# Cross-attention of a decoder layer, from pairs of heads over all tokens to units of one token tile and four heads

## The chip, the cores and the metric

One core of a Trainium2 chip runs the whole program. The time is the device's, in microseconds (us), from launch to end; the kernel before took 972.54 us (median of 3 runs, 971.64 to 976.59). The engines are PE (TensorE: products; PEld is its weight load), DVE (VectorE), ACT (ScalarE), POOL (GpSimd) and SP, which here only issues DMAs. Each engine runs its own list in order, and waits on semaphores that the others raise.

## The reference

Two sequences of 1024 tokens with 256 features pass through one decoder layer: self-attention, cross-attention on 77 context tokens and a feed-forward part, each followed by a residual sum and a layernorm without gain. The cross-attention is the part concerned:

```
q = (x @ Wq.T + bq)          # 1024 x 256, as 16 heads of 16
k = (ctx @ Wk.T + bk)        # 77 x 256
v = (ctx @ Wv.T + bv)
scores = einsum('blhd,bLhd->bhlL', q, k) / sqrt(16)
scores = where(mask, scores, -inf)       # mask 1024 x 77, all ones here
attn = softmax(scores)
out = einsum('bhlL,bLhd->blhd', attn, v) @ Wo.T + bo
x = layernorm(x + out)
```

Keys and queries are carried as two parts (hi and lo, each rounded for the fast fp32r product), so that a score is hi*hi + hi*lo + lo*hi.

## The kernel before

The two sequences (q = 0 and 1 in the code) go through the same stages one after the other: projections (stage Q), self-attention (S), cross-attention (X), norm tail (N), and the feed-forward products (F). The order of every engine's work is written out by hand: each engine walks over the same numbered steps, and in a step does its share of each part. The self-attention works on pairs of heads and chunks of 512 queries. The feed-forward products of sequence 0 are spread over the stages of sequence 1 by the table PLAN, those of sequence 1 stand at the end with a part in its norm tail. They use four PSUM banks for sequence 0 and six for sequence 1 (F_BANKS). The first feed-forward layers (w1, w2) of either sequence's first half stand in the last five steps of its own norm tail, from FFN_STEP to X_END.

Between self-attention and feed-forward stand, for each sequence:

- the norm of the self-attention, tile of 128 tokens by tile: transpose of the result (`y_to_features`), product with w_proj (`project_out`), residual, statistics and norm on DVE with the power on POOL, transpose (`x_to_features`), product with w_q (`project_q`). Tiles 0 to 3 stand beside the last steps of self-attention, tiles 4 to 7 behind it, alone.
- the cross-attention proper, in 9 leading steps and 8 main ones. In a leading step the queries of one pair of heads are split (DVE, POOL), turned by 8 transposes (`x_turn`), evacuated by ACT, multiplied with the keys once to get each query's maximum (`x_max`: a mask product and 8 products of 156 columns, in three groups), reduced on DVE (`x_reduce`), and the negated maximum is turned (`x_rows`) and written by four small DMAs into spare rows of the turned queries, so that the second product of queries and keys already holds the difference. A main step is 4 heads by 512 queries: 4 products (`x_scores`), 4 exponentials on ACT (`x_exps`), the multiplication by the mask on DVE and POOL (`x_mask`), 4 products with the values (`x_values`), an evacuation on DVE, 4 transposes (`x_y_turn`) and the division (`y_norm`).
- the norm of the cross-attention, tiles 0 to 7, which starts beside the last two main steps, and ends in the norm tail.

At the very start DVE waits for the table of cosines and the first projection and then rotates queries and keys (`rope`). The semaphore w_in counts the DMAs of the later weights; DVE, POOL and PE wait for it before self-attention.

Of the kernel before, what the change touches and what calls it, by code (L numbers as in the profile page):

```python
# [109 lines left out]
def norm_step(t):  # L110

    return (y_step(2 * NG - 2) if t < NT // 2 else FINAL_STEP - NT // 2) + 1 + t


S_END = norm_step(NT - 1) + 5
# [12 lines left out]
XSTAGE, XTURN, XMAX, XROWS = 9, 8, 7, 6  # L128
XLAST = NC * NG
XROUNDS = []  # L130
for _s in range(-XSTAGE, XLAST + 2):
    XROUNDS += [("turn", _s + XTURN, i) for i in range(2) if 0 <= _s + XTURN < NP]
    XROUNDS += [("rows", _s + XROWS, 0)] if 0 <= _s + XROWS < NP else []
    XROUNDS += [("y", _s - 2, 0)] if 0 <= _s - 2 < XLAST else []
    if _s == 0:
        XEARLY = len(XROUNDS)
XROUND_AT = {r: n for n, r in enumerate(XROUNDS)}
XUNITS = [(0, 3), (3, 3), (6, 2)]
XSHARED = 3 * XMAX
XNORM = NG + 2  # L140
FFN_STEP = XNORM + NT // 2 + 3
X_END = XNORM + NT + 4


PER = dict(
    x_t_in=16, ctx_in=80, x_in=16, rows_in0=64 * NG, rows_in1=64 * NG, xrows_in0=64 * NG, xrows_in1=64 * NG,
    filled=3, qk_mm=NT, v_mm=NT, rope_mul=3 * NT, rope_add=NT, v_evac=NT,
    ctx_mm=2, ctx_add=2, ctx_stage=3, ctx_turn=2, ctx_evac=4,
# [5 lines left out]
    xstage_hi=NP, xstage_lo=NP, xround_mm=len(XROUNDS), xturn_evac=2 * NP, xrows_evac=NP, xy_norm=2 * XLAST,  # L154
    xmax_mm=3 * NP, xmax_red=3 * NP, xmax_op=2 * NP, xscore_mm=4 * XLAST, xexp_done=4 * XLAST,
    xmask_dve=2 * XLAST, xmask_pool=2 * XLAST, xav_done=XLAST, xy_evac=XLAST,
# [13 lines left out]
XSHARED_BANKS = 6  # L170
F_BANKS = ((2, 3, 4, 5), (0, 1, 2, 3, 4, 5))


def norm_bank(k, what, t):


    if k == 0:
        if t < NT // 2:
            return {"yt": 0, "proj": 1, "xt": 0, "q": 1}[what]
        return {"yt": 0, "proj": 2, "xt": 4, "q": 6}[what] + t % 2  # L180
    return {"yt": 0, "proj": 1, "xt": 0}[what] + (6 if t >= NT // 2 else 0)


def norm_stages(k, s):

    first = [XNORM + t if k else norm_step(t) for t in range(NT)]
    lags = {"yt": 0, "proj": 1, "xt": 3} | ({} if k else {"q": 4})
    return [(what, t) for what, lag in lags.items() for t in range(NT) if first[t] + lag == s]


def bank_before(k, what, t):

    uses = [u for s in range(S_END) for u in norm_stages(k, s)]
    uses = [u for u in uses[:uses.index((what, t))] if norm_bank(k, *u) == norm_bank(k, what, t)]
    return uses[-1] if uses else None
# [11 lines left out]
SLOTS = [("N", 0, s) for s in range(FFN_STEP, X_END)] + [("Q", 1, t) for t in range(NT + V_LAG)] + \  # L207
        [("S", 1, s) for s in range(FIRST_STEP, S_END)] + [("X", 1, s) for s in range(-XSTAGE, FFN_STEP)] + \
        [("N", 1, s) for s in range(FFN_STEP, X_END)] + [("F", 1, j) for j in range(ALONE)]
# [5 lines left out]
    (0, 0, ("w1", "w2"), ("N", 0, FFN_STEP), ("N", 0, X_END - 1)),  # L215
# [7 lines left out]
    (1, 0, ("w1", "w2"), ("N", 1, FFN_STEP), ("N", 1, X_END - 1)),  # L223
# [48 lines left out]
def decoder_layer(nc, a):  # L272
    with ExitStack() as ctx:
# [7 lines left out]
        bias_q = sb("bias_q", [P, D], F32)  # L281
# [9 lines left out]
        xmask_t = sb("xmask_t", [P, T], BF16)  # L291
        kx_t = sb("kx_t", [P, NP, 2 * CP], F32R)
# [28 lines left out]
        def both(name, shape, dt, offset):  # L321
# [18 lines left out]
        kx_tok = both("kx_tok", [P, NP, 2, DH], F32, O_P + 13312)  # L340
        bias_kv = both("bias_kv", [P, 2, D], F32, O_P + 14336)
# [3 lines left out]
        qx_t = [[at(q, f"qx_t{i}", [P, T], F32R, O_T + 4096 * i if i < 6 else O_QK + 8192 + 4096 * (i - 6)) for i in range(NP)]  # L345
                for q in range(BATCH)]
# [5 lines left out]
        xmask_t_u8 = at(0, "xmask_t_u8", [CTX, T], U8, O_T + 4096)  # L352
# [28 lines left out]
        for n in "check_op flag_mm flag_set".split():  # L381
# [12 lines left out]
            x_tok=x_tok, xmask_bias=xmask_bias, xmask_t=xmask_t, xmask_t_u8=xmask_t_u8, xmask_u8=xmask_u8, y_sb=y_sb, y_t=y_t)  # L394
# [4 lines left out]
def build_layer(block, L, S):  # L399
# [41 lines left out]
    def consumer(q, rounds, n, prefix):  # L441

        kind = rounds[n][0]
        count = sum(r[0] == kind for r in rounds[:n + 1])
        name = prefix + {"turn": "turn_evac", "rows": "rows_evac", "y": "y_norm"}[kind]
        return S[name], PER[name] * q + count * (2 if kind == "y" else 1)

    def f_bank(q, n):

        return bank[F_BANKS[q][n % len(F_BANKS[q])]]  # L450

# [14 lines left out]
    def _(sp):  # L466
# [4 lines left out]
        def load_context(q):  # L471
# [4 lines left out]
            for i, n in enumerate(("bk", "bv")):  # L476
                sp.dma_start(L["bias_kv"][q][:, i], a[n].rearrange("(o n) -> o n", o=1).to_broadcast([P, D])).then_inc(S["ctx_in"], 16)
# [33 lines left out]

# [45 lines left out]
        for s in range(-XSTAGE, XLAST):  # L557
            cross_attention(0, s)
# [1091 lines left out]
```

## Time and profile before

| | |
|---|---|
| median of 3 runs | 972.54 us (971.64 to 976.59) |
| the profiled execution | 977.12 us, its span 975.2 us |
| mean granted TensorE clock | 0.914 |
| PE busy | 875.0 us (90%) |
| DVE busy | 547.5 us (56%) |
| ACT busy | 362.9 us (37%) |
| POOL busy | 361.6 us (37%) |

The span is the time from the first to the last instruction. A clock of 1.00 is 2.4 GHz, one of 0.50 is 1.2 GHz. A product's duration in the profile holds its latency too, so products in a row overlap: what one costs in a row is the distance between starts. PE is busy for nine tenths of the span, so time is gained where PE has less to do, waits less, or runs at the higher clock.

### The profile page before, as it was taken

How to read it: one execution, taken by the hardware profiler on the slowest of the kernel's cores; microseconds unless marked ns; L12 is line 12 of the kernel's file. 1: busy time of each engine (PE TensorE's matmuls, PEld its weight loads, DVE VectorE, ACT ScalarE, POOL GpSimd, SP SyncE). 2: the span in 40 equal slices, each digit the busy share in tenths (PEclk: the TensorE clock that was granted, in tenths of full speed). 3: DMA queues.
4: the chain of work that ended last, by engine and by line, in shares of the span. 5: the costliest groups of instructions: out<-in, count | busy, mean ns of one | idle time of the engine just before them, and what ended most of it. 6: DMA issues, size and time to landing. Idle time of an engine off the chain costs nothing.

```text
span 975.2 us, 13106 instructions
## 1 busy us (share of the span) xinstructions
PE 875.0 (90%) x4466; PEld 562.2 (58%) x4466; DVE 547.5 (56%) x1404; ACT 362.9 (37%) x770; POOL 361.6 (37%) x575
## 2 busy tenths in 40 slices
PE   5879999898889799989898899999988989999996
PEld 2544444234734567877666664443457367888785
DVE  4597888677676442235433488884258664117113
ACT  0315666463353322114111146665725433122110
POOL 4312323346445343424222232241343535335332
PEclk9957999769976999999999999997999599999999
DMA  9909101002200123224222105440000000000000
GB/s 330 313 5 398 56 2 45 23 1 72 96 5 0 51 98 112 93 80 152 86 87 87 44 23 183 186 153 2 1 1 6 2 1 0 1 1 23 1 1 24
DMA packets 24955, 69.37 MB, mean 71 GB/s; under 512 B 4539, under 2 KB 12680, under 8 KB 24712
## 3 DMA queue, kind: packets, MB, share of 16 engines
q1 hardware_dynamic: 24888, 68.50, 20.5%
q8 instruction: 39, 0.64, 0.3%
q14 instruction: 28, 0.23, 0.1%
HBM read 65.87 MB, written 13.63 MB: 82 GB/s over the span
## 4 chain that ended last, share of the span: by engine, by line
PE 72%; DVE 17%; POOL 4%; issue 3%; ACT 3%; DMA 1%; SPq 0%; DVEq 0%; POOLq 0%; ACTq 0%
PE bank L892 23%; PE bank L685 7%; PE bank L702 7%; PE bank L654 6%; PE bank L880 4%; DVE bank L1215 4%; DVE max_raw L1213 4%; PE bank L587 3%; PE bank L889 3%; PE bank L825 3%; PE bank L640 2%; PE bank L775 2%; PE bank L735 2%; PE bank L596 1%; POOL prob_s L1501 1%
## 5 line engine op out<-in xcount | busy, mean ns | idle before, releaser
L1530 POOL TENSOR_TENSOR hid_lo_s<-act_raw_s,hid_hi_s 128x512 fp32r<-128x512 f32 x96 | 124.0, 1292 | 211.2 <-DVE hid_hi_s L1392 186.4
L1041 ACT ACTIVATE prob_s<-bank 128x512 f32<-128x512 f32 (+3 forms) x384 | 163.7, 496 | 97.5 <-PE bank L685 97.2
L654 PE MATMUL bank<-k_t_s,q_t_s 64*128 64x512 f32 (+3 forms) x384 | 143.0, 465 | 23.0 <-DVE max_raw L1215 14.9
L1501 POOL TENSOR_SCALAR_AFFINE_SELECT prob_s<-prob_s 128x128 f32<-128x128 f32 x256 | 83.7, 345 | 164.9 <-ACT prob_s L1041 162.5
L1392 DVE CAST hid_hi_s<-act_raw_s 128x512 fp32r<-128x512 f32 x64 | 30.5, 477 | 199.5 <-ACT act_raw_s L1087 199.3
L1215 DVE CUSTOM_DVE_ANT_0 bank<-bank,causal_bf 128x128 f32<-128x128 f32 (+3 forms) x256 | 122.8, 509 | 16.9 <-PE bank L654 14.6
L685 PE MATMUL bank<-q_t_s,k_t_s 64*128 64x512 f32 (+3 forms) x384 | 118.9, 421 | 1.5 <-DVE resid_f_s L1356 0.6
L1087 ACT ACTIVATE act_raw_s<-bank,scales 128x512 f32<-128x512 f32 x64 | 43.8, 689 | 178.4 <-PE bank L892 178.4
L685 PEld LDWEIGHTS bank<-q_t_s,k_t_s 64*128 64x128 f32 x384 | 60.5, 201 | 79.5 <-ACT prob_s L1041 47.9
L654 PEld LDWEIGHTS bank<-k_t_s,q_t_s 64*128 64x128 f32 x384 | 65.6, 205 | 67.8 <-DVE max_raw L1215 31.4
L1213 DVE TENSOR_REDUCE max_raw<-bank 128x1 f32<-128x512 f32 x128 | 82.2, 683 | 39.8 <-PE bank L654 39.8
L892 PE MATMUL bank<-hid_hi_s,home_s 128*128 128x512 f32 x256 | 100.0, 391 | 3.6 <-POOL hid_lo_s L1530 3.5
L892 PE MATMUL bank<-hid_lo_s,home_s 128*128 128x512 f32 x256 | 99.6, 389 | 0.0
L702 PE MATMUL bank<-prob_s,v_sb_s 128*32 128x512 f32 (+3 forms) x768 | 91.4, 551 | 8.0 <-POOL prob_s L1501 7.7
L892 PE MATMUL bank<-hid_hi_s,ring_s 128*128 128x512 f32 x192 | 77.8, 405 | 0.0
L892 PE MATMUL bank<-hid_lo_s,ring_s 128*128 128x512 f32 x192 | 76.6, 399 | 0.0
L892 PEld LDWEIGHTS bank<-hid_hi_s,home_s 128*128 128x128 f32 x256 | 48.0, 188 | 15.4 <-issue 5.6
L892 PEld LDWEIGHTS bank<-hid_lo_s,home_s 128*128 128x128 f32 x256 | 48.1, 188 | 9.8
L1561 POOL TENSOR_TENSOR prob_s<-prob_s,xmask_t 77x512 f32<-77x512 f32 x32 | 39.1, 1240 | 35.4 <-ACT prob_s L1071 35.4
L1071 ACT ACTIVATE prob_s<-bank 77x512 f32<-77x512 f32 x64 | 32.7, 591 | 25.9 <-PE bank L813 25.8
L587 PE MATMUL bank<-w_qkv,x_t_s 128*128 128x512 f32 x64 | 32.2, 636 | 11.1 <-DMA w_qkv<-in_w_qkv 10.3
L1236 DVE COPY y_sb_s<-bank 128x512 f32<-128x512 f32 x32 | 22.1, 689 | 35.5 <-PE bank L702 17.9
(152 smaller groups left out, 1509.6 us busy)
## 6 DMA issues: line engine op xcount, KB each, us to landing
ring_s<-scratch SPq DMA_DIRECT2D x34, 512.0 KB, 3.3
home_s<-scratch SPq DMA_DIRECT2D x22, 512.0 KB, 6.0
checked_s<-scratch SPq DMA_DIRECT2D x3, 3584.0 KB, 21.6
ring_moved_s<-scratch SPq DMA_DIRECT2D x10, 512.0 KB, 3.3
x_t_s<-in_x_t SPq DMA_DIRECT2D x2, 1024.0 KB, 5.7
x_tok_s<-in_x SPq DMA_DIRECT2D x2, 1024.0 KB, 8.0
out<-tok SPq DMA_DIRECT2D x16, 128.0 KB, 1.7
q_t_s<-max_rows SPq DMA_DIRECT2D x64, 4.0 KB
```

What stands on the lines that cost most here:

```text
L587: i = mm(bank[QK_BANKS[q][t % 2]][:], x_t[q][:, k, P * t:P * (t + 1)], L["w_qkv"][:, k, 0:2 * D], start=k == 0, stop=k == KD - 1)
L654: mm(out[:, 0:k1 - k0], qkt(q, p, 0)[r, P * qt:P * (qt + 1)], qkt(q, p, 1)[r, k0:k1], start=True, stop=True).then_inc(S["max_mm"], 1)
L685: mm(S_BANK[j][:, 0:CHUNK - q0], qkt(q, p, 1)[r, P * kb:P * (kb + 1)], qkt(q, p, 0)[r, CHUNK * c + q0:CHUNK * (c + 1)], start=True, stop=T ...
L702: m = mm(Y[32 * j:32 * (j + 1), q0:CHUNK], v_window(v_sb[q][:, kb], 4 * g + j), prob[q][4 * (s % 2) + j][:, 0:CHUNK - q0], start=kb == 0, ...
L892: o = mm(out[:], view(tile_h(f_weights(q, n, 0)[:], k), True), view(src[part][:, k]), start=i == 0, stop=i == last)
L1041: act.activation(prob[q][4 * (s % 2) + j][:, 0:n], S_BANK[j][:, 0:n], ACT.Exp, scale=SCALE).then_inc(S["exp_done"], 1)
L1087: act.activation(act_raw[q][r % 3][:], f_bank(q, n)[:], ACT.Gelu, scale=scales[:, 1 + LAYER_NUMBER[layer], m:m + 1]).then_inc(S["f_act"], 1)
L1213: dve.tensor_reduce(dst, out[:], AXX, ALU.max).then_inc(S["max_red"], 1)
L1215: dve.tensor_tensor_reduce(out=out[:, 0:left], in0=out[:, 0:left], in1=L["causal_bf"][:, CHUNK - left:CHUNK], scale=1.0, scalar=NEG, op0=A ...
L1501: pool.affine_select(out=pr, in_=pr, compare_op=ALU.is_ge, fill=0.0, base=0, pattern=[[1, P]], channel_multiplier=-1).then_inc(S["select_d ...
L1530: pt(dst[1][:, m], act_raw[q][r % 3][:], dst[0][:, m].bitcast(F32), ALU.subtract).then_inc(S["f_lo"], 1)
L1561: pt(pr, pr, L["xmask_t"][0:CTX, CHUNK * (s // NG):CHUNK * (s // NG + 1)], ALU.mult).then_inc(S["xmask_pool"], 1)
```

## The change

The cross-attention works by query tiles. A unit is one token tile (128 queries) and four heads. There are 32 units for each sequence, and a step per unit. The keys are laid out once as block-diagonal matrices (`kx_blocks`, hi and lo, 64 rows by 4 x 78 columns), so that one product of the feature-major queries (64 rows, 128 queries) gives the scores of four heads, 312 columns, with the queries on the partitions. A unit is:

- PE: one mask product of 312 columns and three products (hi*hi, hi*lo, lo*hi) of 312 columns (`x_unit`)
- DVE: the maximum over each head's 77 columns, and the subtraction of it from PSUM into SBUF (`x_softmax`)
- PE, two steps later: 4 transposes of 128x77 (`x_turn`); ACT: one exponential of 77x512 (`x_exp`)
- PE, four steps later: 4 products with the values, 128 columns each (`x_values`)
- for every tile, four units: an evacuation on ACT, 4 transposes (`x_y_turn`), the division on DVE (`x_y_norm`).

The queries come feature-major out of `project_q` (four products of 128 columns instead of two of 256), and are split once, ACT writing hi and POOL lo. The leading steps, the second scores product, the rows of maxima with their DMAs and the multiplication of probabilities by the mask are gone. A query without any allowed key gets its not-a-number from `no_key`, added in the residual. The norm of the self-attention for tiles 4 to 7 stands in steps 0 to 7 of the cross-attention, and the norm of the cross-attention follows every fourth step, from step 11. The norm stages share the banks 0 and 1; the feed-forward products use four banks for both sequences. The w1 and w2 products of a sequence's first half stand in steps 33 to 43 (11 steps in place of 5). At the start the later weights' semaphore counts nine DMAs (bias and block tables are new among them), and DVE and POOL wait for it before the first rotation.

```diff
-XSTAGE, XTURN, XMAX, XROWS = 9, 8, 7, 6
-XLAST = NC * NG
-XUNITS = [(0, 3), (3, 3), (6, 2)]
-XNORM = NG + 2
-FFN_STEP = XNORM + NT // 2 + 3
-X_END = XNORM + NT + 4
+XN = NT * NG
+XTURN, XVALUES, XY = 2, 4, 2 * NG + 1
+X_NORM = XY + 2
+FFN_STEP = XN + 1
+X_END = NG * (NT - 1) + X_NORM + 5
+def norm_stages(stage, s):
+    first = {(0, t): NORM_STEP + t for t in range(NT // 2)} if stage == "S" else \
+            {(0, t): t - NT // 2 for t in range(NT // 2, NT)} | {(1, t): NG * t + X_NORM for t in range(NT)}
+    lags = {"yt": (0, 0), "proj": (1, 1), "xt": (3, 4), "q": (4, None)}
...
-F_BANKS = ((2, 3, 4, 5), (0, 1, 2, 3, 4, 5))
+XUNIT_BANKS = (2, 3)
+XTURN_BANKS = (4, 5)
+F_BANKS = (2, 3, 4, 5)
+NORM_BANKS = {"yt": 0, "xt": 0, "proj": 1, "q": 1}
...
@@ sync @@
-        for dst, name in ((L["bias_q"], "bq"), (L["bias_o"], "bo"), (L["scale_w3"], "s3")):
+        for dst, name in ((L["bias_o"], "bo"), (L["scale_w3"], "s3")):
...
-        sp.dma_start(scales[:], a["scales"]).then_inc(w_in, 16)
+        for dst, name in ((scales, "scales"), (L["bq_t"], "bq_t"), (L["bk_t"], "bk_t"), (L["blocks"], "blocks")):
+            sp.dma_start(dst[:], a[name]).then_inc(w_in, 16)
...
-        for s in range(-XSTAGE, XLAST):
-            cross_attention(0, s)
@@ tensor @@
-            for i in range(KD):
-                m = mm(out[:, 0:D], x1_t[q][t % 2][:, i], L["w_q"][:, i], start=i == 0, stop=i == KD - 1)
+            for half in range(KD):
+                for i in range(KD):
+                    m = mm(norm_bank("q")[:, P * half:P * (half + 1)], L["w_q"][:, i, P * half:P * (half + 1)], x1_t[q][t % 2][:, i],
+                           start=i == 0, stop=i == KD - 1)
...
+        def x_unit(q, n):
+            t, g = divmod(n, NG)
+            if n == 0:
+                wait(pe, q, "ctx_blocks", 4)
+                wait(pe, q, "exp_done", 4 * LAST)
+            if g == 0:
+                wait(pe, q, "q_hi", t + 1)
+                wait(pe, q, "q_lo", t + 1)
+            if n >= 2:
+                wait(pe, q, "xsub", n - 1)
+            out = x_bank(XUNIT_BANKS, n)[:, 0:4 * CP]
+            mask = L["xmask_bias"][:, t].unsqueeze(1).to_broadcast([P, 4, CP])
+            mm(out.rearrange("p (j k) -> p j k", k=CP), L["ident_bf"][:], mask, start=True, stop=False)
+            half, r = g // 2, slice(SLOT * (g % 2), SLOT * (g % 2 + 1))
+            for i, (of_q, of_k) in enumerate(((0, 0), (0, 1), (1, 0))):
+                m = mm(out, xq_hl[q][of_q][r, half, P * t:P * (t + 1)], kx_blocks[of_k][r, half].rearrange("p j k -> p (j k)"), start=False, stop=i == 2)
+            m.then_inc(S["xunit_mm"], 1)
+        def x_turn(q, n):
+            wait(pe, q, "xsub", n + 1)
+            if n >= 2:
+                wait(pe, q, "xexp_done", n - 1)
+            out = x_bank(XTURN_BANKS, n)
             for j in range(4):
+                m = pe.transpose(out[0:CTX, P * j:P * (j + 1)], xdiff[q][n % 4][:, j, 0:CTX], ident[:])
+            m.then_inc(S["xturn_mm"], 1)
+        def x_values(q, n):
+            t, g = divmod(n, NG)
+            wait(pe, q, "xexp_done", n + 1)
+            if n == 0:
+                wait(pe, q, "y_evac", 2 * NG)
+            elif g == 0:
+                wait(pe, q, "xy_evac", t)
             for j in range(4):
+                m = mm(Y[32 * j:32 * (j + 1), P * g:P * (g + 1)], v_window(vx[0:CTX], 4 * g + j),
+                       prob[q][n % 4][0:CTX, P * j:P * (j + 1)], start=True, stop=True)
+            m.then_inc(S["xav_done"], 1)
...
         def f_bank_free(q, n):
-            n -= len(F_BANKS[q])
+            n -= len(F_BANKS)
             if n < 0:
+                wait(pe, q, "xexp_done", XN)
                 return
...
         def cross_attention(q, s, slot=None, exact=True):
+            if s < XN:
+                x_unit(q, s)
+            if 0 <= s - XTURN < XN:
+                x_turn(q, s - XTURN)
+            norm_products(q, "X", s, ("yt", "proj"))
             f_products(slot, exact)
+            if 0 <= s - XVALUES < XN:
+                x_values(q, s - XVALUES)
+            if s >= XY and (s - XY) % NG == 0 and (s - XY) // NG < NT:
+                x_y_turn(q, (s - XY) // NG)
+            norm_products(q, "X", s, ("xt", "q"))
@@ vector @@
+        def x_softmax(q, n):
+            src = x_bank(XUNIT_BANKS, n)[:, 0:4 * CP].rearrange("p (j k) -> p j k", k=CP)[:, :, 0:CTX]
+            wait(dve, q, "xunit_mm", n + 1)
+            dve.tensor_reduce(xmax[:, n % 2], src, AXX, ALU.max).then_inc(S["xmax_red"], 1)
+            wait(dve, q, "xmax_red", n + 1)
+            if n >= 4:
+                wait(dve, q, "xturn_mm", n - 3)
+            tt(xdiff[q][n % 4][:, :, 0:CTX], src, xmax[:, n % 2].unsqueeze(2).to_broadcast([P, 4, CTX]), ALU.subtract).then_inc(S["xsub"], 1)
...
         dve.wait_ge(L["rope_in"], 16 * 2)
-        dve.wait_ge(set_pool, 10)
+        dve.wait_ge(w_in, 16 * 9)
+        dve.wait_ge(set_pool, 11)
         for t in range(NT):
             projections(0, t)
-        dve.wait_ge(w_in, 16 * 7)
```

Two places show how the instructions stand. The first is PE in the main steps of the cross-attention of sequence 0; before, a step was scores (L813), values (L825) and the transposes of the result (L833), 512 columns each:

```order
L813 MATMUL bank<-qx_t_s_131,kx_t 77x512 x2
L813 MATMUL bank<-qx_t_s_132,kx_t 77x512 x2
L825 MATMUL bank<-prob_s_89,vx 32x512
L825 MATMUL bank<-prob_s_90,vx 32x512
L825 MATMUL bank<-prob_s_91,vx 32x512
L825 MATMUL bank<-prob_s_92,vx 32x512
L833 MATMUL bank<-ident,y_sb_s_101 128x128 x4
```

The same engine and place now, from the middle of the 32 steps; L739 and L742 are the unit (mask and three products), L752 the transposes of the unit two steps back, L693 the product with w_o of one tile's norm, L763 the values of the unit four steps back:

```order
L685 MATMUL bank<-ident,tok 128x128 x2
L763 MATMUL bank<-prob_s_88,vx 32x128 x4
L739 MATMUL bank<-xmask_bias,ident_bf 128x312
L742 MATMUL bank<-kx_blocks_hi,xq_hi_s_137 128x312
L742 MATMUL bank<-kx_blocks_lo,xq_hi_s_137 128x312
L742 MATMUL bank<-kx_blocks_hi,xq_lo_s_138 128x312
L752 MATMUL bank<-ident,xdiff_s_143 77x128 x4
L693 MATMUL bank<-w_o,y_t_s_123 128x256 x2
L763 MATMUL bank<-prob_s_85,vx 32x128 x4
```

The norm's products, which stood in a row behind the attention, now stand between a unit and the values of an older one.

The second place is DVE at the start of the program, before the first rotation (L1163 before). In brackets stand the semaphores on which an instruction waits:

```order
L1444 MEMSET xmask_bias 128x312
L1448 TENSOR_SCALAR xmask_bias<-xmask_u_s_155 128x8x77 [waits set_dve,mask_in]
L1449 CAST xmask_t<-xmask_t_u_s_156 77x1024
L1163 TENSOR_TENSOR rope_a_s_103<-bank,cos_t 128x512 [waits qk_mm,set_pool,rope_in]
L1164 TENSOR_TENSOR rope_b_s_107<-bank,sin_t 128x32x8
```

And now, with the rotation at L1084:

```order
L1338 MEMSET xmask_bias 128x312
L1342 TENSOR_SCALAR xmask_bias<-xmask_u_s_157 128x8x77 [waits set_dve,mask_in]
L1344 TENSOR_REDUCE no_key<-xmask_bias 128x8 [waits set_dve]
L1346 TENSOR_SCALAR no_key<-no_key 128x8 [waits set_dve]
L1084 TENSOR_TENSOR rope_a_s_103<-bank,cos_t 128x512 [waits set_pool,qk_mm,w_in,rope_in]
L1085 TENSOR_TENSOR rope_b_s_107<-bank,sin_t 128x32x8
```

The wait for w_in has moved from behind the eight rotations to ahead of the first.

## Rows read from the trace of the kernel before

**Rows 1.** Windows by stage: busy of PE, PEld, DVE, ACT, POOL; clock, DMA

```profile
238.20:345.40 107.20, 89.43 (x468) 57.58 (x467) 70.99 (x164) 42.40 (x88) 47.34 (x60) 0.86 0.16 54
715.50:813.30 97.80, 85.69 (x466) 54.95 (x465) 69.30 (x161) 41.69 (x87) 43.44 (x56) 0.88 0.01 2
```

**Rows 2.** Windows: norm of tiles 4-7, leading steps, main steps (both sequences)

```profile
238.20:250.20 12.00, 9.90 (x49) 6.99 (x47) 7.92 (x21) 3.07 (x8) 8.05 (x14) 1.00 0.94 331
250.20:273.80 23.60, 20.27 (x149) 18.29 (x149) 16.93 (x44) 10.57 (x22) 5.59 (x9) 0.93 0.02 5
281.90:308.60 26.70, 26.39 (x107) 9.55 (x104) 16.69 (x33) 13.05 (x26) 14.46 (x12) 0.50 0.00 1
756.10:779.30 23.20, 23.18 (x94) 7.21 (x94) 15.46 (x28) 10.83 (x22) 12.82 (x11) 0.50 0.01 2
```

**Rows 3.** Timeline, PE, leading steps: start, length, what, [idle before]

```profile
262.77 1.19 PE L775 MATMUL bank<-ident,stage_q_s 128*128 128x128 f32 x8
263.80 0.36 PE L789 MATMUL bank<-xmask_bias,ident_bf 128*128 128x468 bf16 x1
263.82 0.63 PE L792 MATMUL bank<-kx_t,qx_t_s 128*128 128x156 f32 x3
264.29 0.37 PE L789 MATMUL bank<-xmask_bias,ident_bf 128*128 128x468 bf16 x1
```

**Rows 4.** Timeline, PE, end of self-attention and its norm

```profile
233.65 0.42 PE L702 MATMUL bank<-prob_s,v_sb_s 128*32 128x128 f32 x8
234.00 0.44 PE L742 MATMUL bank<-ident,tok 128*128 128x128 f32 x2
...
246.16 1.03 PE L752 MATMUL bank<-w_q,x_t_s 128*128 128x256 f32 x4
```

**Rows 5.** Timeline, PE, last main steps, at the higher clock

```profile
308.66 1.06 PE L825 MATMUL bank<-prob_s,vx 77*32 77x512 f32 x8
309.65 0.66 PE L833 MATMUL bank<-ident,y_sb_s 128*128 128x128 f32 x4
310.15 0.38 PE L728 MATMUL bank<-ident,tok 128*128 128x128 f32 x2
310.37 1.03 PE L735 MATMUL bank<-w_o,y_t_s 128*128 128x256 f32 x4
```

**Rows 6.** Chain of waits, w1 products: start, length, what

```profile
320.59 3.24 PE bank L880 x13
```

**Rows 7.** Groups of DVE, 238.2 to 345.4 us: busy, mean ns, idle before

```profile
L1236 DVE COPY y_sb_s<-bank 128x512 f32<-128x512 f32 x8 | 5.5, 689 | 9.0 <-PE bank L833 9.0
L1312 DVE TENSOR_REDUCE max_raw<-bank 128x4 f32<-128x308 f32 x8 | 3.8, 471 | 0.0
L1250 DVE TENSOR_TENSOR tok<-bank,recip 128x256 f32<-128x256 f32 x8 | 3.4, 424 | 0.3
```

**Rows 8.** Groups of ACT, 281.9 to 308.6 us

```profile
L1071 ACT ACTIVATE prob_s<-bank 77x512 f32<-77x512 f32 x24 | 12.3, 591 | 11.8 <-PE bank L813 11.8
```

**Rows 9.** Timeline, PE, first hidden layer of sequence 1

```profile
817.47 0.47 PE L892 MATMUL bank<-hid_hi_s,home_s 128*128 128x512 f32 x1 [0.94 <-POOL hid_lo_s L1530]
```

**Rows 10.** Start of the program: SP's issue, its landing, DVE's first rotation, PE

```profile
10.52 1.13 SPq L539 DMA_DIRECT2D scales<-in_scales  x1
...
DMA to landing us min/median/max: 7.6/7.6/7.6
...
14.20 0.69 DVE L1163 TENSOR_TENSOR rope_a_s<-bank,cos_t 128x512 f32<-128x512 f32 x1 [5.87 <-PE bank L587]
...
10.00:38.00 28.00, 26.22 (x82) 14.81 (x83) 14.20 (x33) 6.07 (x13) 10.13 (x8) 1.00 1.07 356
```

**Rows 11.** Timeline, PE, main steps, at the lower clock

```profile
293.13 1.12 PE L833 MATMUL bank<-ident,y_sb_s 128*128 128x128 f32 x4
294.18 1.13 PE L813 MATMUL bank<-qx_t_s,kx_t 64*77 64x512 f32 x4
```

**Rows 12.** Window: maxima of the self-attention's first pairs of heads

```profile
45.00:86.00 41.00, 35.63 (x125) 19.32 (x124) 33.91 (x113) 11.52 (x23) 5.41 (x12) 0.51 0.40 149
```

More of the change, by code:

```diff
@@ L169, with norm_before @@
 SHARED = (6, 2)
-XSHARED_BANKS = 6
-F_BANKS = ((2, 3, 4, 5), (0, 1, 2, 3, 4, 5))
[L174 to L194, printed above, removed]
+XUNIT_BANKS = (2, 3)
+XTURN_BANKS = (4, 5)
+F_BANKS = (2, 3, 4, 5)
+NORM_BANKS = {"yt": 0, "xt": 0, "proj": 1, "q": 1}
+def norm_before(what, k, t):
+    uses = [u for name, steps in (("S", S_END), ("X", X_END)) for s in range(steps) for which in (("yt", "proj"), ("xt", "q"))
+            for u in norm_stages(name, s) if u[0] in which]
+    uses = [u for u in uses[:uses.index((what, k, t))] if NORM_BANKS[u[0]] == NORM_BANKS[what]]
     return uses[-1] if uses else None
@@ L432, in unit_bank, with x_bank, norm_bank, consumer @@
         return bank[n % SHARED[q]] if n < 2 * NU else A_BANK[n % 2]
-    def x_unit_bank(n):
-        return bank[n % XSHARED_BANKS] if n < XSHARED else A_BANK[n % 2]
+    def x_bank(banks, n):
+        return bank[banks[n % 2]]
+    def norm_bank(what):
+        return bank[NORM_BANKS[what]][:, 0:D]
     def v_window(v, h):
         return v[:, VW * h:VW * h + 32]
[L441 to L445, printed above, removed]
+    def consumer(q, n):
+        kind = ROUNDS[n][0]
+        count = sum(r[0] == kind for r in ROUNDS[:n + 1])
+        name = {"turn": "turn_evac", "rows": "rows_evac", "y": "y_norm"}[kind]
         return S[name], PER[name] * q + count * (2 if kind == "y" else 1)
-    def f_bank(q, n):
-        return bank[F_BANKS[q][n % len(F_BANKS[q])]]
+    def f_bank(n):
+        return bank[F_BANKS[n % len(F_BANKS)]]
     def ring_tile(r):
@@ L837, in f_bank_free, with x_y_turn @@
+        def x_y_turn(q, t):
+            wait(pe, q, "xy_evac", t + 1)
+            if t:
+                wait(pe, q, "xy_norm", 2 * t)
+            else:
+                wait(pe, q, "y_norm", 4 * NG)
+            for g in range(NG):
+                m = pe.transpose(R[:, P * g:P * (g + 1)], y_sb[q][:, P * g:P * (g + 1)], ident[:])
+            m.then_inc(S["xy_mm"], 1)
         def f_bank_free(q, n):
-            n -= len(F_BANKS[q])
+            n -= len(F_BANKS)
             if n < 0:
+                wait(pe, q, "xexp_done", XN)
@@ L860, in f_product @@
             c, layer, m = GROUPS[n]
-            out, last = f_bank(q, n), 3 if layer in ("w1", "w2") else 15
+            out, last = f_bank(n), 3 if layer in ("w1", "w2") else 15
             k, part = i // 2, i % 2
@@ L1002, in _, with evac_round @@
     def _(act):
[L1003 to L1006 removed]
+        def evac_round(q, key, out, name, rows=P, columns=CHUNK):
+            wait(act, q, "round_mm", ROUND_AT[key] + 1)
+            src = round_bank(ROUND_AT[key])[0:rows, 0:columns]
+            act.activation(out, src, ACT.Copy).then_inc(S[name], 1)
         def v_evac(q, t):
@@ L1136, in _ @@
         act.wait_ge(S["check_op"], PIECES + 3)
-        for s in range(-XSTAGE, FFN_STEP):
+        for s in range(FFN_STEP):
             cross_attention(0, s)
@@ L1581, in _ @@
         pool.memset(low_bits[:], 0).then_inc(S["check_op"], 1)
-        for t in range(NT):
+        pool.wait_ge(w_in, 16 * 9)
+        for t in range(NT + 1):
             projections(0, t)
-        pool.wait_ge(w_in, 16 * 7)
         for s in range(FIRST_STEP, S_END):
@@ L1588, in _ @@
         fill(1)
-        for s in range(-XSTAGE, FFN_STEP):
+        for s in range(FFN_STEP):
             cross_attention(0, s)
```

571 lines of the change are left out of this document (211 added, 360 removed).

## The prediction, made before the changed kernel ran

> **What bounds the kernel now.** I read the windows by stage first. The change lies between two points that both kernels have: the first transpose of the norm of tile 4, and the end of the first w1/w2 products. For sequence 0 that is 107.2 us, for sequence 1 it is 97.8 us [rows 1]; all else but the start keeps its order. In both stretches PE is the busiest, 89.4 of 107.2 us and 85.7 of 97.8 us, DVE has about 70, ACT 42, at a mean granted clock of 0.86 and 0.88. The windows inside them say where it goes [rows 2]: 12.0 us for four tiles of norm alone, 23.6 us of leading steps in which PE (20.3) and DVE (16.9) are both near full, and 26.7 us of main steps in which PE is never idle (26.4) but is granted 0.50. Sequence 1 repeats it (23.2 us at 0.50). So PE's own work, its clock in the main steps, and waits in the thin parts bound these stages, in that order; I read the timeline of PE for what each kind of product costs in a row, and DVE's groups for whether it could keep up.
>
> **The change part by part.** I price the new stage by PE's list, at the higher clock, from starts of neighbouring rows.
>
> *A unit.* Before, a group of 468 mask columns and three products of 156 takes 264.29 - 263.80 = 0.49 us for 936 columns in four instructions [rows 3]. The new unit has four instructions too, with 1248 columns. 312 more columns at 2.4 GHz are 0.13 us: 0.62 us. Products of 64 rows by 312 columns stand nowhere in the trace; if the weight loads bound them it is 0.49, if columns scale as a whole 0.49 x 1248/936 = 0.65. I take 0.62, near the upper one.
>
> *Its turn.* Eight transposes take 263.80 - 262.77 = 1.03 us [rows 3], so four take 0.52. The new ones load 77 columns instead of 128 and stream the same 128; they could cost less, hardly more: 0.40 to 0.52, I take 0.52.
>
> *Its values.* Four products of 128 columns take 234.00 - 233.65 = 0.35 us (with their last latency 0.42) [rows 4]. I take 0.35.
>
> Sum 1.49 us a unit; 32 units are 47.7 us.
>
> *Once a tile.* The four transposes of the result take 310.15 - 309.65 = 0.50 us; two transposes and the product with w_o or w_proj take 0.22 + 1.03 = 1.25 us, counted to the end of the latter's latency [rows 5]; a second pair of transposes, at most the same 0.22 with 0.1 us of change-over, 0.32; the product with w_q 1.03 us [rows 4], with the same columns now in twice as many instructions. Eight tiles of cross-attention and four of self-attention: 8 x 0.50 + 12 x 1.25 + 12 x 0.32 + 4 x 1.03 = 27.0 us.
>
> *The w1/w2 products.* 13 take 3.24 us [rows 6], so 64 take 16.0 us, as before.
>
> *A wait at step 33.* The first w1 product takes a bank that the last exponential frees; PE has just made its turn, so it waits about one exponential, 0.59 us [rows 8], with its hand-over 0.7 us.
>
> Together 47.7 + 27.0 + 16.0 + 0.7 = 91.4 us for each sequence, so 107.2 - 91.4 = 15.8 us less for sequence 0 and 6.4 us less for sequence 1. Behind the latter, two waits of 0.94 us for POOL's lo part stand in the first hidden layer (the first of them [rows 9]); with w1 and w2 spread over 11 steps instead of 5, POOL is done by then. That is 1.9 us more.
>
> *Does anything else set the step?* DVE has a reduction of 308 columns, 0.47 us, and a subtraction of 308: by 256 columns 0.42 and 512 columns 0.69 it is 0.42 + 0.27 x 52/256 = 0.48 us [rows 7]. With two hand-overs 1.05 us a unit. A tile's norm costs it 7.92/4 = 2.0 us [rows 2], the division at most 2 x 0.42: 0.7 us a step in the middle of the stage, 1.75 us in all, against PE's 1.49 + (0.50 + 1.25 + 0.32)/4 = 2.0 us. In steps 0 to 7 PE has a whole norm with w_q beside the unit, some 4 us, and DVE 1.05 + 2.0. The turn waits for a subtraction of two steps before, the values for an exponential of two steps before (0.59 us), the banks of the units for the same subtraction; all of it has a step's room. What is late next is PE itself. ACT loses the 16 evacuations and POOL its multiplications; they hide nothing and were hidden. The 32 small DMAs of the maxima of each sequence go from SP's queue and nothing new queues there.
>
> *The four banks of sequence 1.* ACT's and DVE's work on one group of 512 columns (0.69 us each, by the copy [rows 7]) lies well under the four groups of 1 us (4 x 0.25 [rows 6]) that PE works ahead. I cost it at nothing; if it shows, it is some tenths per w1/w2 pair, 16 pairs, up to 3 us.
>
> *The start.* DVE's first rotation stands at 14.20 us, when PE's first projection ends. It now waits for all nine DMAs of w_in. SP issues the scales at 10.52 us, and they land 7.6 us later [rows 10]; three issues more than before behind it and three less ahead of it, so the last lands about 19 us, and DVE starts 5 us late. Queued behind the rotation are all others, POOL's additions with them, and PE may run two tiles ahead, with the context's products in between; its third tile, at about 18 us, slips to about 20.7. PE is busy 26.2 of the 28 us there [rows 10], so little of it is regained; 0.9 us of transposes of the keys go. Between 0 and 5 us, I take 2 us.
>
> Sum: -15.8 - 6.4 - 1.9 + 2 = -22.1 us. The profiled run took 977.12 us, 4.6 us above the median of 972.54; the difference, taken from the median, gives 950.4 us. Bounds: 64 units x (-0.25 to +0.03) us are -16 to +2; the start -2 to +3 about the 2 us taken; banks 0 to +3; unpriced change-overs of a tenth a step 0 to +6. That is 932 to 964, mostly inside 940 to 960.
>
> **The clock.** All of this is at 1.00. The old main steps ran at 0.50 although PE was never idle there [rows 2], and there four transposes take 294.18 - 293.13 = 1.05 us [rows 11] against 0.50 above. So PE's being busy does not keep the clock; what it is busy with matters. Against the new mix: its products use 64 or 77 of the rows, as those at 0.50 did, and the maxima of the first pairs in self-attention, also 64 rows with transposes between, ran at 0.51, with 5.4 of 41 us idle [rows 12]. For it: the leading steps, a mask product, products of 156 columns and transposes, were granted 0.93 in spite of waits, and each norm that now stands between units is the kind of work that ran at 1.00 [rows 2]. The values' share, the largest part of the old main steps, falls to a quarter of a unit. I think it keeps the higher clock, but this is the doubt that carries the range.
>
> In the leading steps 64 transposes, 8.2 us at 0.129, are 40% of PE's 20.3 busy us, and the clock was 0.93 [rows 2, 3]. In the new middle steps 0.52 + (0.50 + 0.22 + 0.32)/4 = 0.78 of 2.0 us are transposes, 39%. The Trainium skill (TensorE: Matmul & The Clock Gate, Part 4: PE-mode transpose) says that a transpose does not count as busy for the clock gate in the way that a product does. The trace speaks against taking that as decisive at this share; if the rule decided, the outcome would be the first rival's.
>
> **The rivals.** *The clock falls (slower).* Place: steps 8 to 31, behind the heavy norms. Every kind of work there costs about twice (1.05 against 0.50): 2.0 more us a step. All 48 steps: 950 + 96 = 1046 us; half of them, 998. It loses the gain from 11 steps on (22/2.0). For it and against it stands above.
>
> *DVE or the round trip sets the step.* If the hand-overs are 0.3 us and not 0.05, or the norm's chain holds the banks 0 and 1 (a transpose now waits until the evacuation and DVE's subtraction behind the previous one are done, where norms had more banks), a step takes 2.3 us: 64 x 0.3 = 19 us, 970 us, which is no change. Against: DVE is under 1.75 us and the bank's two users stand a step apart.
>
> *The norms do not hide.* PE's list is in order, so they cost PE the same; this would only matter if they waited. It is in the range.
>
> *The start costs more.* If nine DMAs land past 22 us, 5 us more: 955 us.
>
> **How the numbers follow.** Forecast 0.78, with its own range 938 to 962. The clock falls 0.13 (of this a third ends above 1000 us, and a little, with few steps, near 970). DVE or the round trip 0.06. The late start 0.03, still faster. What the measurement of this kernel can tell from no change is about 0.5%, 967.7 to 977.4 us. Of the clock's 0.13 I put 0.11 above that band and 0.02 in it, of DVE's 0.06 half in it and half below. Faster 0.78 + 0.03 + 0.03 = 0.84, same 0.02 + 0.03 = 0.05, slower 0.11. The range of 8 in 10 is 936 to 970: it leaves some 3% below, and above it most of the clock's case.
>
> **What would show it.** Right: from the first unit to the end of the w1/w2 products PE is busy over 95% at a clock of 1.00, steps in the middle of 2.0 us, units 0.62 us apart from their turn, the stage 89 to 94 us in both sequences; the first rotation at about 19 us. Wrong: a clock of 0.50 in the middle steps; idle time of PE before L739 or L752 put down to DVE's subtraction, or before L685 put down to the norm; more than a tenth of idle time in the start beyond 3 us.

## The result, and the profile after

| | before | after |
|---|---|---|
| median, 20 runs each | 974.96 us | 967.63 us |
| ratio to before | | 0.994 (95% interval 0.992 to 0.996) |
| the profiled execution, its span | 977.12, 975.2 us | 965.38, 963.7 us |
| stage of sequence 0, granted clock | 107.2 us, 0.86 | 102.7 us, 1.00 |
| stage of sequence 1, granted clock | 97.8 us, 0.88 | 101.0 us, 1.00 |

The ratio and its interval are taken from the fast runs alone: one run before and two after were in a slower state of the chip.

Faster by 0.6%, about a quarter of the 2.3% forecast (by the medians 7.3 us of 22.1): inside the wide range of 936 to 970 us and outside the likeliest case's own, 938 to 962. The two windows that answer to [rows 1] are these (window, length, then busy us and instructions of PE, its weight loads, DVE, ACT and POOL, granted clock, DMA share and GB/s):

```profile
235.10:337.80 102.70, 97.75 (x741) 67.03 (x739) 65.84 (x156) 39.63 (x79) 26.58 (x44) 1.00 0.16 54
702.40:803.40 101.00, 97.28 (x738) 66.80 (x738) 64.56 (x153) 38.69 (x76) 23.26 (x40) 1.00 0.01 1
```

PE is busy for 95% and 96% of them, at 1.00. The clock came out as forecast and the busy share just so, and the stages are still 11.3 and 9.6 us longer than the 91.4 us that I had summed. So most of the fault is in what PE's own list costs. Its timeline in the middle of the stage (start, length, what) shows one step and the next:

```profile
298.26 0.30 PE L739 MATMUL bank<-xmask_bias,ident_bf 128*128 128x312 bf16 x1
298.50 0.41 PE L742 MATMUL bank<-kx_blocks_hi,xq_hi_s 64*128 64x312 f32 x1
298.74 0.30 PE L742 MATMUL bank<-kx_blocks_lo,xq_hi_s 64*128 64x312 f32 x1
298.88 0.30 PE L742 MATMUL bank<-kx_blocks_hi,xq_lo_s 64*128 64x312 f32 x1
299.12 0.66 PE L752 MATMUL bank<-ident,xdiff_s 128*77 128x128 f32 x4
299.71 0.42 PE L763 MATMUL bank<-prob_s,vx 77*32 77x128 f32 x8
300.07 0.31 PE L739 MATMUL bank<-xmask_bias,ident_bf 128*128 128x312 bf16 x1
```

The unit takes 299.12 - 298.26 = 0.86 us where I had 0.62 and an upper bound of 0.65. The turn takes 0.59 (I had 0.52), the values 0.36 (0.35). Between the second and third key product there are 0.14 us, which is 312 columns at 2.4 GHz plus 0.01. Three gaps are longer, 0.24 us each: from mask to first key product, from first to second, and from the last to the turn. The first and the last of them stand where the number of rows goes from 128 to 64 and back. The middle one doesn't, and it is still there, 0.25 us, in the first experiment, which has no change of rows; so it is no part of what follows. The weight loads of the same step show the other two:

```profile
298.16 0.10 PEld L739 LDWEIGHTS bank<-xmask_bias,ident_bf 128*128 128x128 bf16 x1
298.49 0.18 PEld L742 LDWEIGHTS bank<-kx_blocks_hi,xq_hi_s 64*128 64x128 f32 x1 [0.24 <-issue]
298.60 0.19 PEld L742 LDWEIGHTS bank<-kx_blocks_lo,xq_hi_s 64*128 64x128 f32 x1
298.75 0.18 PEld L742 LDWEIGHTS bank<-kx_blocks_hi,xq_lo_s 64*128 64x128 f32 x1
299.12 0.43 PEld L752 LDWEIGHTS bank<-ident,xdiff_s 128*77 128x77 f32 x4 [0.19 <-issue]
```

And these are the groups of weight loads of the whole stage (after the bar: busy us, mean ns of one, idle time before them and what ended it):

```profile
L752 PEld LDWEIGHTS bank<-ident,xdiff_s 128*77 128x77 f32 x128 | 13.9, 147 | 6.0 <-issue 6.0
L742 PEld LDWEIGHTS bank<-kx_blocks_hi,xq_hi_s 64*128 64x128 f32 x32 | 5.8, 183 | 6.4 <-issue 4.4
L763 PEld LDWEIGHTS bank<-prob_s,vx 77*32 77x32 f32 x256 | 5.1, 108 | 7.2 <-issue 5.2 <-ACT prob_s L1001 2.0
L739 PEld LDWEIGHTS bank<-xmask_bias,ident_bf 128*128 128x128 bf16 x32 | 3.1, 97 | 2.7 <-issue 2.4 <-DVE xdiff_s L1231 0.2
```

"Issue" is idle time in which the loads waited for nothing that the profile shows. The second key product's load (298.60) runs under the first key product, whereas the first load of 64 rows (298.49) starts 0.23 us behind the start of the mask product (298.26), and the first load back at 128 rows (299.12) 0.24 us behind that of the last key product (298.88). This view was there for the kernel before too; a row of it, 272 to 345 us, may be the same sign, 10.8 us ahead of 32 loads that follow the 32-column values products. Its size is no price of a change, for those loads wait behind products of 512 columns, most of them at the clock of 0.50 [rows 2]:

```profile
L833 PEld LDWEIGHTS bank<-ident,y_sb_s 128*128 128x128 f32 x32 | 5.1, 198 | 11.6 <-issue 10.8 <-DVE y_sb_s L1236 0.8
```

A second loss is a wait in five steps of each sequence, 2.4 us in all. It is the two users of bank 0 of which I had written that they "stand a step apart":

```profile
302.12 0.37 ACT L973 ACTIVATE y_t_s<-bank 128x256 f32<-128x256 f32 x1
302.63 0.41 PE L701 MATMUL bank<-ident,tok 128*128 128x128 f32 x2 [0.47 <-ACT y_t_s L973]
```

**Where the profile's 11.5 us of span went.** The stages gave 4.5 and took 3.2. The tail behind them gave 1.6, with one wait for the lo part, 0.58 us, in place of two of 0.94 [rows 9]. The self-attentions, whose code is the same but for the norm beside their last steps, gave 2.9 and 4.7 us; the start and the projections of sequence 1 gave the last 1.0. Here is the self-attention of sequence 1, before, after, and in e4_no_mask below, in windows that are rounded to 1 us; from its first turn to the end it is 275.5, 270.8 and 278.7 us:

```profile
439.00:715.00 276.00, 256.27 (x1376) 154.00 (x1376) 158.99 (x462) 121.44 (x267) 89.11 (x190) 0.94 0.26 89
```

```profile
432.00:702.00 270.00, 247.26 (x1380) 148.46 (x1378) 157.86 (x459) 122.49 (x270) 90.11 (x192) 0.97 0.26 91
```

```profile
430.00:708.00 278.00, 256.43 (x1383) 153.62 (x1381) 157.65 (x459) 122.26 (x269) 90.32 (x192) 0.94 0.25 88
```

Over the nine profiled executions of the changed kernel and its variants it lasted 268.3 to 278.7 us, with the same instructions and a mean clock of 0.99 to 0.94. The 4.7 us lie inside that spread, so one profile of each kernel can't show them to be an effect of the change. The same spread can account for the profiles' differing by 11.7 us where the medians differ by 7.3. For it the experiments below are read by their stages: from the first unit's first key product to the first projection of the next sequence (or the first hidden layer), 102.3 and 100.7 us for the changed kernel.

### The profile page after: what moved, and what is told of

Its sections match the earlier page's. It is cut to its first block, busy times and chain, and to the rows that moved or that the text cites. A ratio compares the mean times of both kernels' runs of the same rounds, so it can differ in the third digit from the quotient of the medians.

```text
span 963.7 us, 14216 instructions
## 1 busy us (share of the span) xinstructions
PE 878.7 (91%) x5034; PEld 576.5 (60%) x5034; DVE 535.0 (56%) x1385; ACT 354.5 (37%) x746; POOL 328.0 (34%) x554
## 4 chain that ended last, share of the span: by engine, by line
PE 74%; DVE 14%; POOL 4%; issue 4%; ACT 2%; SPq 1%; DMA 0%; POOLq 0%; DVEq 0%; ACTq 0%
PE bank L833 23%; PE bank L643 6%; PE bank L661 6%; PE bank L612 6%; PE bank L821 4%; DVE max_raw L1131 4%; PE bank L742 4%; DVE bank L1133 4%; PE bank L752 4%; PE bank L830 3%; PE bank L693 3%; PE bank L598 2%; PE bank L556 2%; PE bank L763 2%; POOL prob_s L1398 2%
## 5 line engine op out<-in xcount | busy, mean ns | idle before, releaser
L612 PE MATMUL bank<-k_t_s,q_t_s 64*128 64x512 f32 (+3 forms) x384 | 138.4, 451 | 25.7 <-DVE max_raw L1133 16.4
L643 PE MATMUL bank<-q_t_s,k_t_s 64*128 64x512 f32 (+3 forms) x384 | 115.7, 416 | 2.0 <-issue 1.2
L612 PEld LDWEIGHTS bank<-k_t_s,q_t_s 64*128 64x128 f32 x384 | 63.5, 199 | 70.3 <-DVE max_raw L1133 31.3
L833 PE MATMUL bank<-hid_hi_s,home_s 128*128 128x512 f32 x256 | 99.9, 390 | 0.6 <-POOL hid_lo_s L1427 0.6
L833 PE MATMUL bank<-hid_lo_s,home_s 128*128 128x512 f32 x256 | 99.6, 389 | 0.0
L661 PE MATMUL bank<-prob_s,v_sb_s 128*32 128x512 f32 (+3 forms) x768 | 88.7, 536 | 10.5 <-POOL prob_s L1398 10.3
L833 PE MATMUL bank<-hid_hi_s,ring_s 128*128 128x512 f32 x192 | 78.0, 406 | 0.0
L833 PE MATMUL bank<-hid_lo_s,ring_s 128*128 128x512 f32 x192 | 76.8, 400 | 0.0
L1001 ACT ACTIVATE prob_s<-bank 77x512 f32<-77x512 f32 x64 | 37.9, 593 | 77.6 <-PE bank L752 77.6
L1405 POOL TENSOR_SCALAR ln_var<-ln_mean 128x1 f32<-128x1 f32 x32 | 9.7, 302 | 137.3 <-DVE ln_mean L1194 137.2
L833 PEld LDWEIGHTS bank<-hid_hi_s,home_s 128*128 128x128 f32 x256 | 48.1, 188 | 11.4 <-issue 1.4
L833 PEld LDWEIGHTS bank<-hid_lo_s,home_s 128*128 128x128 f32 x256 | 48.0, 188 | 9.9
L752 PE MATMUL bank<-ident,xdiff_s 128*77 128x128 f32 x256 | 42.2, 287 | 0.2 <-issue 0.2
```

Source lines behind the costliest of these rows:

```text
L612: mm(out[:, 0:k1 - k0], qkt(q, p, 0)[r, P * qt:P * (qt + 1)], qkt(q, p, 1)[r, k0:k1], start=True, stop=True).then_inc(S["max_mm"], 1)
L643: mm(S_BANK[j][:, 0:CHUNK - q0], qkt(q, p, 1)[r, P * kb:P * (kb + 1)], qkt(q, p, 0)[r, CHUNK * c + q0:CHUNK * (c + 1)], start=True, stop=T ...
L661: m = mm(Y[32 * j:32 * (j + 1), q0:CHUNK], v_window(v_sb[q][:, kb], 4 * g + j), prob[q][4 * (s % 2) + j][:, 0:CHUNK - q0], start=kb == 0, ...
L752: m = pe.transpose(out[0:CTX, P * j:P * (j + 1)], xdiff[q][n % 4][:, j, 0:CTX], ident[:])
L833: o = mm(out[:], view(tile_h(f_weights(q, n, 0)[:], k), True), view(src[part][:, k]), start=i == 0, stop=i == last)
```

## The experiments

All times in us; the stages are read from one profile of each. e6_values_no_wait and e7_values_pairs have one run each and no interval.

| run | median | ratio to before (95%) | stage 0 | stage 1 |
|---|---|---|---|---|
| after | 967.6 | 0.994 (0.992 to 0.996) | 102.3 | 100.7 |
| e1_full_rows | 949.1 | 0.972 (0.968 to 0.976) | 92.0 | 90.3 |
| e2_act_order | 971.4 | 0.996 (0.992 to 0.999) | 100.9 | 99.3 |
| e3_values_rows | 969.1 | 0.994 (0.992 to 0.997) | 102.2 | 100.7 |
| e4_no_mask | 964.2 | 0.987 (0.982 to 0.992) | 96.8 | 95.3 |
| e5_rows_act | 948.7 | 0.976 (0.972 to 0.979) | 90.6 | 89.0 |
| e6_values_no_wait | 952.2 | | 91.7 | 90.3 |
| e7_values_pairs | 939.3 | | 86.4 | 85.1 |
| e8_best | 934.8 | 0.959 (0.956 to 0.963) | 85.2 | 83.8 |

**Key products over all 128 rows.** Each group of four heads gets its own block of keys, zero in the other group's rows. The products have the same columns and compute the same sums, for 5 KB more a partition and four more small multiplications a sequence on POOL. (In the code below, `...` stands for lines and arguments that are not shown.)

```diff
-kx_blocks = [sb(f"kx_blocks_{n}", [P, KD, 4, CP], F32R) ...]
+kx_blocks = [sb(f"kx_blocks_{n}", [P, NG, 4, CP], F32R) ...]
-m = mm(out, xq_hl[q][of_q][r, half, tile], kx_blocks[of_k][r, half], ...)
+m = mm(out, xq_hl[q][of_q][:, g // 2, tile], kx_blocks[of_k][:, g], ...)
```

> The three key products of a unit take all 128 rows of the array instead of 64: a block of keys per group of heads that is zero in the rows of the other group (twice the bytes, the same columns, the same result). Theory A (the 0.85 us of a unit against my 0.62 is a weight load that stays uncovered wherever the products change from 128 to 64 rows and back): the unit falls to 0.60 to 0.68 us, the stage of sequence 0 from 102.7 us to about 96, that of sequence 1 from 101.0 to about 95, the whole by 11 to 15 us (ratio to before 0.979 to 0.983). Rival B (it is the change from the bf16 mask to the fp32r keys, or the fp32r product itself): the unit stays at 0.83 to 0.87 us, the ratio at 0.994. Rival C (rows that carry more data cost more power): the granted clock falls below 1.00 in these stages and the ratio is at or over 1.

The direction is theory A's, the size beyond the 6 to 7 us a stage that I had expected: 10.3 and 10.4 us. The timeline of the same place:

```profile
302.12 0.30 PE L739 MATMUL bank<-xmask_bias,ident_bf 128*128 128x312 bf16 x1
302.14 0.41 PE L741 MATMUL bank<-kx_blocks_hi,xq_hi_s 128*128 128x312 f32 x1
302.39 0.30 PE L741 MATMUL bank<-kx_blocks_lo,xq_hi_s 128*128 128x312 f32 x1
302.53 0.31 PE L741 MATMUL bank<-kx_blocks_hi,xq_lo_s 128*128 128x312 f32 x1
302.68 0.60 PE L751 MATMUL bank<-ident,xdiff_s 128*77 128x128 f32 x4
303.21 0.43 PE L762 MATMUL bank<-prob_s,vx 77*32 77x128 f32 x8
```

The first key product now starts 0.02 us behind the mask product, and the turn 0.15 us behind the last key product. The unit takes 0.56 us, inside the bounds of the prediction, and its turn 0.53. The weight loads lost the idle time that they had:

```profile
L751 PEld LDWEIGHTS bank<-ident,xdiff_s 128*77 128x77 f32 x128 | 16.1, 146 | 0.5 <-issue 0.5
L741 PEld LDWEIGHTS bank<-kx_blocks_hi,xq_hi_s 128*128 128x128 f32 x32 | 6.2, 195 | 0.4
```

"Issue" falls from 6.0 + 4.4 = 10.4 us to 0.5, the stage by 10.3. Twice the rows for the same columns cost nothing and left the clock at 1.00, against rival C; the change from bf16 to fp32r is still there, against rival B. 10.3 us over 64 changes of rows is 0.16 us each. Its window has PE busy for 86.7 us where the changed kernel's had 97.8:

```profile
239.40:331.40 92.00, 86.71 (x739) 67.63 (x737) 64.35 (x156) 39.55 (x79) 26.58 (x43) 1.00 0.18 61
```

**ScalarE's order.** The evacuation of y_t stands ahead of the exponential of its step.

```diff
 def cross_attention(q, s):
+    for what, k, t in norm_stages("X", s):
+        if what == "yt":
+            yt_evac(q, k, t)
     x_exp(q, s - XTURN)
-    norm_evacs(q, "X", s)
+    for what, k, t in norm_stages("X", s):
+        if what == "xt":
+            xt_evac(q, k, t)
...
```

> ScalarE evacuates y_t ahead of the exponential of the same step instead of behind it; nothing else. Theory A on the waits (TensorE stands 0.47 us once per token tile ahead of x_to_features because bank 0 is still being read by the y_t evacuation, which stands behind a 0.59 us exponential): those waits go, 5 in sequence 0 and about as many in sequence 1, 2.4 us each sequence, the time by 3 to 5 us (ratio 0.989 to 0.991). Rival (the exponential that is now late is waited for by the values or the next turn): the waits reappear at the values or at the turn, ratio 0.993 to 0.996.

The waits fell from 0.47 to 0.21 us in the main steps, 2.4 to 1.0 us in sequence 0, and the stages by 1.4, where I had expected the waits to go whole. Of the rival, that they come back elsewhere, there is 0.2 us more of idle time ahead of a turn. What is left seems to be the evacuation itself, 0.37 us. The whole-kernel ratio can't tell 1.4 us a stage from nothing: it came out at 0.996, and its interval, 0.992 to 0.999, overlaps that of the changed kernel.

**Values over 128 rows.** The rows of the values beyond the 77 keys are zero.

```diff
-m = mm(Y[...], v_window(vx[0:CTX], 4 * g + j), prob[q][n % 4][0:CTX, ...], ...)
+m = mm(Y[...], v_window(vx[:], 4 * g + j), prob[q][n % 4][:, ...], ...)
```

> The values products of cross-attention contract over all 128 rows instead of 77, with the value rows beyond the 77 keys at zero; same columns, same result. Theory A (a change of the number of rows uncovers a weight load): a turn followed by values falls from 0.59 to 0.50 us and the mask behind the values is loaded ahead, 0.1 to 0.2 us a step, 3 to 6 us a sequence, ratio 0.982 to 0.988. Rival B (what counts is the wait on a semaphore at the first values product and the 32-column output, both kept): no change, ratio 0.994.

Nothing changed, and my theory as I had put it fell: 77 rows or 128 are the same to the array.

**No mask.** The mask product is left out of the unit, so this kernel applies no mask.

```diff
-mm(out.rearrange("p (j k) -> p j k", k=CP), L["ident_bf"][:], mask, start=True, stop=False)
```

> The unit leaves the mask product out, so no mask is applied; the three key products stay at 64 rows. By theory A the first key product's load is still uncovered behind a 128-row product: the unit falls by one pitch of about 0.13 to 0.23 us to 0.62 to 0.72 us, 4 to 7 us a sequence. Rival B (the uncovered part belongs to the change from bf16 to fp32r): the unit falls to 0.50 us or under, 11 us a sequence, ratio about 0.972.

5.5 and 5.4 us a stage, what theory A gives and half of what rival B does. The change of rows did not go with the mask; it only stands behind another product (the groups of this run):

```profile
L750 PEld LDWEIGHTS bank<-ident,xdiff_s 128*77 128x77 f32 x128 | 13.8, 147 | 6.0 <-issue 5.0 <-DVE xdiff_s L1229 0.9
L740 PEld LDWEIGHTS bank<-kx_blocks_hi,xq_hi_s 64*128 64x128 f32 x32 | 5.8, 183 | 5.8 <-issue 4.7 <-DVE xdiff_s L1229 0.5
```

**Both edits.**

> The 128-row units of e1_full_rows with the ScalarE order of e2_act_order. Each stage went from 102.3 to 92.0 us (sequence 0) and from 100.7 to 90.3 us (sequence 1) by the first edit, and by 1.4 us by the second. If the two are independent the stages last 90.6 and 88.9 us and the ratio to before is about 0.969. If the 0.47 us waits return elsewhere now that TensorE is faster, the stages stay at 92 and 90.

The stages add up: 90.6 and 89.0 us. The median of the whole kernel, 948.7 us, doesn't show it beside the 949.1 of e1_full_rows.

**The values without a wait of their own.** Built on e1_full_rows, as the next is.

```diff
-wait(pe, q, "xexp_done", n + 1)
+if n + XVALUES - XTURN >= XN:
+    wait(pe, q, "xexp_done", n + 1)
```

> e1_full_rows without the values products' own wait for the exponential: the turn ahead of them in the same step waits for the same count already. Theory A (the first value load, 0.16 us of idle on the weight loads, is held because its instruction waits on a semaphore): the load goes ahead under the turn, 0.1 us or more a step, stages of about 88.5 and 87 us. Rival B (the load is held because the products change from 128-column to 32-column tiles of the array): nothing changes, 92.0 and 90.3 us.

Rival B, in one run: 91.7 and 90.3 us. The load ahead of the values is not held by the semaphore.

**The values in pairs.**

```diff
-if 0 <= s - XVALUES < XN:
+if 0 < s - XVALUES < XN and (s - XVALUES) % 2:
+    x_values(q, s - XVALUES - 1)
     x_values(q, s - XVALUES)
```

> e1_full_rows with the values products of two units together in every other step: half as many changes into and out of the 32-column products. If each pair of changes costs about 0.3 us (0.16 us of idle ahead of the first value load, 0.20 us ahead of the mask's), 16 pairs fewer give 4 to 5 us a sequence: stages of about 87.5 and 86 us. If what is uncovered belongs to each group of values whatever stands ahead of it: 92.0 and 90.3 us.

About 5.5 and 5.2 us less than e1_full_rows, where I had expected 4 to 5, with every product unchanged. Not all of it is changes of shape. PE is busy for 4.2 us less in sequence 0 (86.7 to 82.5) and 4.1 in sequence 1, and the rest is waiting: the waits for bank 0 fell from 2.4 to 1.3 us, and one of 0.5 us ahead of the values gave way to one of 0.5 ahead of the product with w_q. Sixteen groups of values fewer have 32 changes fewer, so that is 0.13 us each, less than the price found for the rows. e8_best against e5_rows_act is the same edit, with six timed runs of each: in their profiles PE is again busy for 4.1 us less in either sequence (86.5 to 82.4 and 86.2 to 82.0). The window and the weight loads of this run:

```profile
236.90:323.30 86.40, 82.47 (x736) 69.53 (x736) 63.80 (x156) 39.44 (x78) 26.54 (x43) 1.00 0.18 64
```

```profile
L762 PEld LDWEIGHTS bank<-prob_s,vx 77*32 77x32 f32 x256 | 6.0, 109 | 3.0 <-issue 2.9 <-ACT prob_s L1001 0.2
L739 PEld LDWEIGHTS bank<-xmask_bias,ident_bf 128*128 128x128 bf16 x31 | 3.0, 98 | 0.4 <-issue 0.2
```

**All three.**

> All three: 128-row units, ScalarE order, values in pairs. If they add up: stages of about 86 and 84.5 us, ratio to before 0.960 (0.956 to 0.966). If pairs bring nothing: 90.6 and 88.9 us, ratio 0.969.

The windows of its two stages:

```profile
237.70:322.90 85.20, 82.39 (x738) 69.68 (x736) 63.90 (x156) 39.42 (x78) 26.58 (x43) 1.00 0.18 66
689.80:773.50 83.70, 81.86 (x736) 69.50 (x735) 62.61 (x153) 38.44 (x76) 23.22 (x40) 1.00 0.01 1
```

This version beats both kernels: 4.1% under the one before, and its stages are 0.7 us or so below what I had expected. It makes the same matrix products as the changed kernel, with more rows in some and in another order.

## Why the prediction was wrong

**The step that failed** is "A unit", with the bound "if columns scale as a whole 0.65". The row that I scaled had a mask product and three key products that all take 128 rows [rows 3], and the new unit's take 64. I had noted that such products stand nowhere in the trace, and bounded them by columns and by weight loads alone. The array's change from one shape to another was in neither bound. It was priced once, as "unpriced change-overs of a tenth a step 0 to +6"; the unit took 0.86 us and not 0.62, and the runs show 0.32 us a step for the change of rows alone, 10.3 us a sequence. Three comparisons carry this: the same unit without the change (e1_full_rows), with a product fewer but the change kept (e4_no_mask), and another change of shape made half as often (e7_values_pairs). What the array does in those 0.16 us no run shows.

The Trainium skill says it outright (TensorEngine Tiling (Array Packing), Key Properties): changing the tiling mode, and not just the tile, drains the array. This case agrees that a change costs time, for two kinds, full to 64 rows at 0.16 us a change and full to 32 columns at 0.13; between 77 rows and 128 nothing changed (e3_values_rows).

The sum of sequence 0, term by term, measured from the start of each product to the start of the next work, waits apart:

| | forecast, us | measured, us |
|---|---|---|
| 32 units | 19.8 | 27.4 |
| 32 turns | 16.6 | 17.6 |
| 32 groups of values | 11.2 | 11.9 |
| once a tile | 27.0 | 24.6 |
| w1/w2 | 16.0 | 16.1 |
| waits | 0.7 | 4.9 |
| sum | 91.4 | 102.5 |

So 7.6 of the 11 us are the units. The waits gave 4.2 more: 2.4 for bank 0, and besides the 0.7 at step 33 one of 1.0 us ahead of the next projection, one of 0.5 ahead of a w1 product, both for DVE, and 0.4 in small ones. The work of a tile cost 2.4 us less, since the products with w_o, w_proj and w_q had been priced with their latency. Without the change of rows (e1_full_rows) the units take 18.3 us and the turns 15.7, both under the forecast, which is why that edit gave more than the 8.5 us by which the two had been priced too low.

Point by point:

- *The clock falls* was wrong: 1.00 in both stages. The stretches at 0.50 [rows 2] are gone. Four steps in the middle took 9.6 us (288.68 to 298.26), 3.2 of them transposes, 34% where I had worked out 39%, and the clock stayed at 1.00.
- *DVE or the round trip sets the step* was wrong in its main clause: DVE is busy 65.8 of 102.7 us, its reduction takes 0.475 and its subtraction 0.478 us, as worked out, and in e8_best the same work fits in 85.2 us. Its second clause, banks 0 and 1 held by the norm, was right in kind: 2.4 us in each sequence, not 19. My argument against it was false, since the first transpose of the next tile and the second of this one stand in the same step, with a 0.59 us exponential between them on ACT.
- The values (0.36 us), the four transposes of the result (0.49), the wait of 0.68 us at step 33 and the stage's busy share were right.
- *The start* cost nothing, where I had taken 2 us. The last of the nine DMAs landed at 16.3 us and not at 19, and the first turn of self-attention stood at 37.65 us against 37.85.
- *The lo part* gave 1.3 us of the 1.9.
- The signs were given as steps of 2.0 us and stages of 89 to 94; the steps were 2.4 us and the stages 102.7 and 101.0.

Not settled is how the remainder of the medians' 7.3 us, behind the stages' 1.3 and the tail's 1.6, divides. The clock of the self-attention moves by more than that from one execution to the next.

## What to carry to other kernels

Price a list of products by the shapes of neighbours too, not by columns alone: mark each place where the rows in use change between 128 and 64, and count 0.16 us, or the columns between 128 and 32, and count 0.13 us, at 2.4 GHz. Other changes were not measured. The sign of it in a profile is idle time of the weight loads put down to "issue", ahead of the first load of the new shape. Here products of 64 rows beside those of 128 were cheaper padded with zeros to 128, and small products of another shape were cheaper in pairs of groups than one group to a step.

## What the hardware showed beside this

- Key products over 64 and over 128 rows cost the same in a row, 0.14 us for 312 columns, and so did values products over 77 and over 128 rows (e3_values_rows).
- The same 128 x 616 conversion of the mask on DVE took 0.48 us after and 3.69 us before. In the one it started at 3.71 us, in the other at 4.04 us, beside POOL's fill of v_sb, 2.0 us long. Why it differs was not tried.
- With unchanged instructions the self-attention of sequence 1 lasted 268 to 279 us in nine profiles, its mean clock 0.99 to 0.94. That is 1% of the whole kernel, more than the 0.6% between the two kernels.
